# Cross-attention kernel: adding the mask and taking the minimum in one VectorE instruction per tile, instead of a mask matmul on TensorE

## The reference, cut to what matters

```python
q   = layernorm(x) @ Wq.T + bq                        # (32, 256, 16*64)
k   = concat([side @ Wk.T + bk, ctx @ Wgk.T + bgk])   # 512 keys
v   = concat([side @ Wv.T + bv, ctx @ Wgv.T + bgv])
att = einsum('bhqd,bhdk->bhqk', q, k) / sqrt(64)
att[..., :256] = where(mask, -inf, att[..., :256])
x   = x + (softmax(att) @ v) @ Wo.T + bo
x   = x + fp8_quantised_gemm(layernorm(x), ffn_kernel) + ffn_bias
```

## Time and profile before

| | us | share of the span |
|---|---|---|
| median of 3 executions (lowest, highest) | 2909.78 (2906.48, 2913.43) | |
| span of the profiled execution, first to last instruction | 2906.8 | |
| PE busy | 2793.8 | 96% |
| PE weight load busy | 2431.0 | 84% |
| DVE busy | 2315.1 | 80% |
| POOL busy | 2099.0 | 72% |
| ACT busy | 1982.3 | 68% |

### The profile page before, as it was taken

The page is one execution under the profiler, slowest core; times in us unless marked ns, Lnnn a source line. Parts: engine busy times, 40 slices in busy tenths (PEclk is TensorE's granted clock), DMA queues, the critical chain, the costliest instruction groups (busy, mean ns, idle before and its releaser), DMA issues.

```text
span 2906.8 us, 68146 instructions
## 1 busy us (share of the span) xinstructions
PE 2793.8 (96%) x20352; PEld 2431.0 (84%) x20352; DVE 2315.1 (80%) x3793; ACT 1982.3 (68%) x4742; POOL 2099.0 (72%) x2504
## 2 busy tenths in 40 slices
PE   5999999999999999999999999999999999999997
PEld 4888888888888888888888888888888888888886
DVE  5888778888778887788887788877888877888776
ACT  4666676766677666767666776667676667766674
POOL 4777777777768777777777687777777776877775
PEclk9999999999999999999999999999999999999998
DMA  5333333333333333333343333333333433333331
GB/s 170 82 77 90 76 86 82 80 79 91 72 90 87 76 90 76 87 83 79 79 92 71 90 87 76 90 77 86 85 79 78 93 69 90 87 76 90 78 82 37
DMA packets 176029, 243.02 MB, mean 84 GB/s; under 512 B 25472, under 2 KB 92544, under 8 KB 176000
## 3 DMA queue, kind: packets, MB, share of 16 engines
q1 hardware_dynamic: 176000, 242.66, 35.6%
HBM read 66.40 MB, written 8.39 MB: 26 GB/s over the span
## 4 chain that ended last, share of the span: by engine, by line
PE 61%; DVE 17%; issue 13%; ACT 7%; DMA 1%; DVEq 1%; POOL 0%; SPq 0%; ACTq 0%; POOLq 0%
PE ps_misc L555 20%; PE ps_o L658 10%; PE ps_pt L645 10%; PE ps_misc L599 8%; PE ps_scores L631 5%; PE ps_scores L632 5%; DVE pt_lo L941 5%; DVE kv_out L912 3%; PE ps_scores L634 2%; ACT probs L786 2%; DVE q_lo L889 2%; DVE scr_b L875 1%; DVE o_t L949 1%; ACT zq_out L751 1%; DVE scr_a L877 1%
## 5 line engine op out<-in xcount | busy, mean ns | idle before, releaser
L481 POOL TENSOR_SCALAR probs<-probs,recips 128x512 f32<-128x512 f32 x1024 | 698.4, 694 | 457.0 <-DVE recips L936 456.8
L795 ACT CAST pt_hi<-ps_pt 128x512 fp32r<-128x512 f32 x1024 | 551.7, 595 | 319.8 <-PE ps_pt L645 314.5
L786 ACT ACTIVATE probs<-ps_scores,neg_max 128x512 f32<-128x512 f32 x1024 | 696.0, 688 | 23.5 <-DVE neg_max L932 11.4
L941 DVE TENSOR_TENSOR pt_lo<-ps_pt,pt_hi 128x512 fp32r<-128x512 f32 x1024 | 655.2, 680 | 53.2 <-ACT pt_hi L795 50.3
L932 DVE TENSOR_REDUCE neg_max<-ps_scores 128x2 f32<-128x1024 f32 x512 | 621.1, 1213 | 9.5 <-PE ps_scores L634 9.5
L658 PE MATMUL ps_o<-pt_hi,v_hl 128*128 128x256 f32 x2048 | 554.6, 302 | 1.0 <-DVE o_t L949 1.0
L645 PE MATMUL ps_pt<-ident,probs 128*128 128x128 f32 x4096 | 531.5, 273 | 1.6 <-DVE pt_lo L941 1.6
L658 PE MATMUL ps_o<-pt_lo,v_hl 128*128 128x256 f32 x2048 | 511.4, 281 | 0.0
L645 PEld LDWEIGHTS ps_pt<-ident,probs 128*128 128x128 f32 x4096 | 464.5, 141 | 8.6 <-POOL probs L481 2.0
L631 PE MATMUL ps_scores<-k_hl,q_hh 128*128 128x512 f32 x1024 | 456.8, 446 | 9.0 <-issue 4.7
L632 PE MATMUL ps_scores<-k_hl,q_lo 128*128 128x512 f32 x1024 | 407.1, 398 | 0.0
(11 more groups left out here) (106 smaller groups left out, 6567.1 us busy)
## 6 DMA issues: line engine op xcount, KB each, us to landing
k_hl<-k_split SPq DMA_DIRECT2D x1024, 128.0 KB, 2.3
mask_sb<-mask_dram SPq DMA_DIRECT2D x128, 256.0 KB, 3.3
q_hh<-q_hh SPq DMA_DIRECT2D x256, 128.0 KB, 2.4
x_sb<-x_dram SPq DMA_DIRECT2D x32, 256.0 KB, 2.8
side_raw<-side_t_dram SPq DMA_DIRECT2D x32, 256.0 KB, 3.6
scr_b<-ctx_t_dram SPq DMA_DIRECT2D x32, 256.0 KB, 2.8
out_dram<-y SPq DMA_DIRECT2D x32, 256.0 KB, 2.1
probs<-wq_t_dram SPq DMA_DIRECT2D x1, 1024.0 KB, 5.1
```

The source lines that it names most:

```text
L481: nc.gpsimd.tensor_scalar(probs[:, h % 2, t, :], probs[:, h % 2, t, :], recips[:, h % 2, t:t + 1], 1.0, ALU.mult, ALU.mult).then_inc(norm_ ...
L786: nc.scalar.activation(probs[:, h % 2, t, :], ps_scores[:, h % 2, t, :], ACT.Exp, bias=neg_max[:, h % 2, t:t + 1], scale=-1.0, accum_out=s ...
L795: nc.scalar.copy(pt_hi[:, h % 2, 2 * k:2 * k + 2, :], ps_pt[:, k, :, :]).then_inc(pthi_done, 1)
L941: V.tensor_tensor(pt_lo[:, h % 2, 2 * k:2 * k + 2, :], ps_pt[:, k, :, :], pt_hi[:, h % 2, 2 * k:2 * k + 2, :].bitcast(F32), ALU.subtract). ...
```

## The change

The mask matmul, its weights and PE's waits for the mask are gone. The minimum is now taken by `tensor_tensor_reduce`, one instruction for each of the two query tiles: it reads the tile's scores (128x512 f32, PSUM) and 512 mask bytes (SBUF), computes `out = (in0 + in1) * MASK_STEP`, writes that back over the scores in PSUM, and writes the minimum of `out` and 3e38 to `neg_max`. For the keys without a mask the second input reads 256 bytes of zeros that stand in one new row behind the mask rows (a pattern of two rows, `row::MASK_ROWS - row`). `w_q` and its bias are scaled by -1/8 / 2**80, so that the instruction's factor 2**80 restores the scores while a mask byte becomes 2**80. `min_done` now rises twice per head, and ACT waits for it tile by tile. DVE waits for the mask of a group before the first head of it, and its wait for the scores stands apart.

```diff
@@ buffers
-        mask_weight = sb("mask_weight", [P, P], BF16)
-        mask_sb = sb("mask_sb", [P, 2, GH * QT * S], U8)
+        mask_sb = sb("mask_sb", [P, MASK_ROWS + 1, S], U8)      # MASK_ROWS = 2 * GH * QT
-        W_SCALE = {"q": SCORE_SCALE}
+        W_SCALE = {"q": SCORE_SCALE / MASK_STEP}                # MASK_STEP = 2.0 ** 80
@@ SP: load_mask
-                    wait_apart(sp, "sp", scores_done, H * b + GH * (n - 1))
+                    wait_apart(sp, "sp", min_done, QT * (H * b + GH * (n - 1)))
@@ PE: scores
-                    mm(dst, q_lo[:, n % 2, i, rows], k_hl[:, n % 2, i, :], start=False, stop=False)
-                    m = mask_sb[:, n % 2, (i * QT + t) * S:(i * QT + t + 1) * S].bitcast(FP8E5)
-                    last = mm(dst[:, 0:S], mask_weight[:], m, start=False, stop=True)
+                    last = mm(dst, q_lo[:, n % 2, i, rows], k_hl[:, n % 2, i, :], start=False, stop=True)
@@ PE: batch
-                            pe.wait_ge(mask_loaded[nxt % 2], 16 * (2 * bb + nxt // 2 + 1))
@@ ACT: exps
-                act.wait_ge(min_done, g + 1)
-                if free:
-                    act.wait_ge(pt_full, 2 * (g - 1))
                 for t in range(QT):
+                    act.wait_ge(min_done, QT * g + t + 1)
+                    if free and t == 0:
+                        act.wait_ge(pt_full, 2 * (g - 1))
@@ DVE: mins
-                dve.wait_ge(scores_done, g + 1)
-                V.tensor_reduce(neg_max[:, h % 2, :], ps_scores[:, h % 2, :, :], AX_X, ALU.min).then_inc(min_done, 1)
+                wait_apart(dve, "dve", scores_done, g + 1)
+                n, i = h // GH, h % GH
+                for t in range(QT):
+                    row = (n % 2 * GH + i) * QT + t
+                    s = ps_scores[:, h % 2, t, :].rearrange("p (k s) -> p k s", s=S)
+                    V.tensor_tensor_reduce(out=s, in0=s, in1=mask_sb[:, row::MASK_ROWS - row, :], scale=MASK_STEP,
+                                           scalar=SCORE_LIMIT, op0=ALU.add, op1=ALU.min,
+                                           accum_out=neg_max[:, h % 2, t:t + 1]).then_inc(min_done, 1)
@@ DVE: prologue and batch
+            V.memset(mask_sb[:, MASK_ROWS, :], 0).then_inc(mask_zeros, 1)
-            V.tensor_scalar(mask_weight[:], ident[:], MASK_WEIGHT, None, ALU.mult)
+            dve.wait_ge(mask_zeros, 1)
+            dve.wait_ge(mask_loaded[0], 16)
+                        if (h + 2) % GH == 0:
+                            nxt = (h + 2) // GH % NG
+                            dve.wait_ge(mask_loaded[nxt % 2], 16 * (2 * (b + (h + 2) // H) + nxt // 2 + 1))
                         mins((h + 2) % H, g + 2)
```

More of the change, by code:

```diff
@@ L27 @@
 BF16 = mybir.dt.bfloat16
-FP8E5 = mybir.dt.float8e5
 U8 = mybir.dt.uint8
@@ L44 @@
 GW = GH * DK
+MASK_ROWS = 2 * GH * QT
 SCORE_SCALE = -1.0 / DK ** 0.5
 LN_EPS = 1e-5
-MASK_WEIGHT = 2.0 ** 116
+SCORE_LIMIT = 3.0e38
+MASK_STEP = 2.0 ** 80
 E4_MAGIC = 1.5 * 2.0 ** 20
@@ L221, in xattn_ffn_kernel @@
         zeros_done = sem("zeros_done")
+        mask_zeros = sem("mask_zeros")
         mask_loaded = [sem("mask_loaded0"), sem("mask_loaded1")]
@@ L302, in load_mask @@
                 if not (isinstance(b, int) and b == 0 and n < 2):
-                    wait_apart(sp, "sp", scores_done, H * b + GH * (n - 1))
+                    wait_apart(sp, "sp", min_done, QT * (H * b + GH * (n - 1)))
                 src = one(mask, b).rearrange("o p n -> (o p) n")
-                sp.dma_start(mask_sb[:, n % 2, :],
-                             src[:, n * GH * QT * S:(n + 1) * GH * QT * S]).then_inc(mask_loaded[n % 2], 16)
+                rows = mask_sb[:, n % 2 * GH * QT:(n % 2 + 1) * GH * QT, :].rearrange("p r s -> p (r s)")
+                sp.dma_start(rows, src[:, n * GH * QT * S:(n + 1) * GH * QT * S]).then_inc(mask_loaded[n % 2], 16)
             def one(ap, b):
@@ L678, in _ @@
             pe.wait_ge(q_placed, Q_PLACES)
-            pe.wait_ge(mask_loaded[0], 16)
             pe.wait_ge(consts_done, 1)
@@ L696, in batch @@
                         if ahead % GH == 0:
-                            bb = b + ahead // H
-                            pe.wait_ge(mask_loaded[nxt % 2], 16 * (2 * bb + nxt // 2 + 1))
                             pe.wait_ge(zq_ready, c.through("q", nxt, ZQ))
@@ L974, in _ @@
             dve.wait_ge(consts_loaded, CONSTS)
-            V.tensor_scalar(qk_bias[:, 0, :], qk_bias[:, 0, :], SCORE_SCALE, None, ALU.mult)
+            V.tensor_scalar(qk_bias[:, 0, :], qk_bias[:, 0, :], SCORE_SCALE / MASK_STEP, None, ALU.mult)
             V.reciprocal(scales[:, 2:4], scales[:, 0:2])
```

## The result

Before takes 2908.53 us (median, 2906.48 to 2913.43), the changed kernel 2924.78 us (2923.71 to 2925.53). The ratio is 1.0054, with an interval of 1.004 to 1.0068: 0.54% slower, 16 us. The forecast was 1.4% slower, 40 us. The sign is right, the size is off by a factor of 2.5, so the experiments went after the terms of the sum.

What follows compares the result with a forecast made beforehand. DVE's chain was taken to bound heads 3 to 10, PE mostly the rest. Per batch 8d - 0.90, with d = 0.27, gives +1.26 us; times 32, +40 us: 2950 us, 1.4% slower, range 2885 to 3020.

Steps and rivals of the forecast that it cites:

- What bounds the kernel: Steady batch: DVE's chain, 98% busy, sets the time in heads 3 to 10; PE is busy all of the rest.
- What is added on DVE: Per head, two new minimum instructions of 0.60 + 0.10 us each replace one reduce of 1.13 us.
- d: Excess on DVE of a head's two new minimum instructions over the old single reduce, forecast 0.27 us.
- The other edits I cost at nothing: Semaphore increment, mask waits on DVE, later mask load, ACT's earlier first exponential, edits outside the loop: 0 us.
- semaphore pair: DVE's separate wait for the scores with its semaphore increment: costed at nothing, in the range at 0.5 us a batch.
- PE's gain: Removed mask matmuls save 0.90 us a batch: 0.21 at head 14's transposes, 0.69 in heads 15, 0 and 2.
- A: Rival: DVE's new instruction brings out its minimum at no cost; 2899 us, or 2881 at the reduce's rate; chance 0.25.
- case of no change: DVE's excess per head between 0.09 and 0.135 us, so that the time doesn't move; chance 0.10.
- B: Rival: PE bounds throughout, DVE's chain has slack, all 118 us of mask matmuls come back: 2792 us; chance 0.04.
- C: Rival: on DVE the minimum's read waits for the main part to end; excess 0.57 per head, 3027 us; chance 0.16.
- D: Rival: the new DVE instruction runs at half rate; excess 2.05 us per head, 3406 us; chance 0.03.
- The signs: PE busy down over 100 us, batch about 90.0, (6,B) wait up some 2 us, new (9,B) wait, minimum distance 1.40.

Runs made afterwards that it cites:

- e1: Kernel before without its mask matmuls, the mask left out of the computation: 2886.47 us, ratio 0.9916.
- e2: Changed kernel with the mask matmuls put back on PE, so the mask is added twice: 2945.31 us, ratio 1.0122.
- e3: Kernel before with two extra 128x2 reciprocals on DVE behind the minimum, in heads 5 to 11 only: 2925.55 us, ratio 1.0057.
- e4: Kernel before with two extra 128x2 reciprocals on DVE behind the minimum, in the nine heads outside 5 to 11: 2910.64 us, ratio 1.0002.
- e5: Kernel before with DVE's wait for the scores set apart with its semaphore increment, instead of the plain wait: 2915.64 us, ratio 1.0028.
- e6: Changed kernel with DVE's waits for mask and scores, and the semaphore increment, put ahead of the reciprocal's own wait: 2908.61 us, ratio 1.0002.
- e11: Changed kernel with mask matmul and plain reduce again for heads 4 to 11, first output's copy moved from head 3 to 13: 2870.63 us, ratio 0.9861.
- e9: Kernel before with DVE's copy of the first output moved from head 3 to head 13: 2884.16 us, ratio 0.9912.

## Why the prediction was wrong in size and right in sign

**What bounds the kernel: right.** Heads 3 to 10 belong to DVE and the rest mostly to PE. e1 and e2 show it from both sides: the stretch takes 41.54 without the mask matmuls and 41.56 with them, and with the new instruction 42.84 either way. e3 against e4 shows it by place. PE's busy share of 96% said the opposite. (The prediction's "PE's 98% in that stretch" is a misreading: 36.98 of 38.62 is 96%, and the 98% is DVE's.)

**The sum: the step that failed is "What is added on DVE", the 0.10 us per tile for bringing the minimum out.** The prediction took 0.60 + 0.10 per tile and d = 0.27. The instruction's timeline gives 1.24 to 1.27 for the two tiles and d = 0.12 in each head: 0.60 to 0.62 for the first tile and 0.65 for the second, with the read inside. The price was taken from the reciprocal's 0.10 as if small instructions add up, and already e3's two reciprocals hold 0.13 together. The Trainium skill, "VectorE: DVE Perf Modes", section "Two Vector instructions with no wait between them", says that such an instruction is two, and the trace agrees (1024 rows of 140 ns). How long the second part holds DVE I took from the reciprocal, and that was four times too large: (1.25 - 1.20) / 2 = 0.025 instead of 0.10. Of 7 x 0.27 = 1.89 in the stretch, 0.85 came.

With d = 0.12 the prediction's own sum is 8 x 0.12 - 0.90 = +0.06 us a batch, 2 us: no change. That isn't what was measured either, and the right sign was in part luck: with the sizes as measured, the kernel is slower by a term that the prediction put at nothing. Two more terms were off:

**"The other edits I cost at nothing": wrong for the semaphore pair, and it seems for the mask's wait in head 6.** The ledger of DVE's starts in heads 3 to 9, before to after: minima 7.93 to 8.78, idle ahead of them 0 to 0.37 (0.08, 0.20 and 0.09 in heads 3, 6 and 8), reciprocals 0.65 to 0.81, all else -0.1 net. The sum is the +1.28 of the stage. The -0.1 is itself a sum of large terms that the prediction doesn't have: +0.44 for the three neighbours in head 3, -0.33 for the normalise in head 9, -0.12 for `q_lo` in head 7, -0.09 for the quantising in head 6. That they nearly cancel is chance. The range had an item for the semaphore pair (0.07 x 7, 0.5 a batch), and that was the better value. e5 shows the pair's cost alone, 7.7 us or +0.27 in the stretch; of the 16 us that e6 gives back, -0.55, only 0.17 is idle time that is gone. The Trainium skill, "VectorE: DVE Perf Modes", section "The DRAIN you can't avoid", reports a chain of eight copies where a semaphore after each one cost nothing. Whether it stood in an instruction of its own the page doesn't say. Here, in e5, a wait and an increment in instructions of their own did cost, and the measurement decides.

**PE's gain: 0.62 to 0.66 a batch instead of 0.90.** e1 has -0.39 and -0.23, after -0.37 and -0.29. By the starts of single heads, 15 and 0 gave about 0.25 each, head 2 only 0.14, heads 13 and 14 together about 0.08 in after. The reason there is the one named, `norm` of head 14 on POOL: in after it ends at 1557.39 and the transposes start at 1557.52, 0.13 later, where the prediction allowed 0.06 for the signal. Why head 2 gave less isn't shown.

```profile
1556.02 1.37 POOL L485 TENSOR_SCALAR probs<-probs,recips 128x512 f32<-128x512 f32 x2
1557.52 1.09 PE L647 MATMUL ps_pt<-ident,probs 128*128 128x128 f32 x8
```

Together: 7d 1.89 became 0.85, nothing for the pair and its neighbours became 0.43 (0.37 + 0.16 - 0.10), and -0.63 (the 0.90, less d in head 12) became -0.66. That is +0.62 for the forecast +1.26.

**The rivals.** A (d = 0.07) is nearer in d than the forecast and has the wrong sign, since it leaves out the waits. The measured 0.12 lies in the case of no change (0.09 to 0.135), which had 0.10, and the distance of 1.24 to 1.27 stands right at the mark of 1.24 below which A was to decide. B is refuted by e1. C and D didn't come: the main part takes 707 ns, near the 680 of `pt_lo`. The row that spoke for D, L882 at 1589 ns, was no rate of its kind: in after the same operation (L881) takes 722 ns, and L879, which took 698 as L880, takes 1532. The Trainium skill's rule on two SBUF sources that aren't bf16 ("Vector Engine (DVE) Microarchitecture Reference", section "Points that are easy to get wrong") isn't borne out by that 722 ns either; both sources there are the same SBUF tile, in f32.

**The signs.** PE's busy time fell by 68 us and not by over 100, with 1024 matmuls fewer. A batch lost 3.7 us of matmuls and became 0.60 longer, so by this estimate PE stood still 4.3 us longer; its recorded idle time grew by 2.67 only. The rest would lie under the recorded ends of the matmuls ahead of a wait, 284 ns long where the next one can start after some 120. PE's wait at (6,B) grew from 0.83 to 1.21 in this batch, not to 2; (9,B), for which a wait was forecast, has 0.07 on average; instead the wait in head 3 grew from 0.16 to 0.59, and head 5 has new ones of 0.65 together. They are waits for DVE's copy. At (8,A), two heads after (6,B), PE waits for ACT, 0.55 (0.31 in before). Here are (6,B), (8,A) and (10,A):

```profile
1519.31 0.39 PE L559 MATMUL ps_misc<-zt_hi,wq_hi 128*128 128x256 f32 x1 [1.21 <-DVE kv_out L911]
1527.30 0.39 PE L559 MATMUL ps_misc<-kv_hi,wk_hi 128*128 128x256 f32 x1 [0.55 <-ACT z L767]
1538.38 0.65 PE L622 MATMUL ps_misc<-ident,scr_a 128*128 128x128 f32 x4 [0.68 <-DVE kv_out L911]
```

Over the run PE's weight loads for these chunks waited 122.5 us for that copy, 52.4 before, and its matmuls 80.6, 32.7 before:

```profile
PEld ps_misc L559 <- DVE kv_out L911: 122.5, 159, 2.5
```

**What stays open.** Why the pair leaves DVE idle in heads 3, 6 and 8 and not in 4, 5, 7 and 9. In heads 3 and 6 the wait just ahead of it, on the exponentials or on an earlier result, is a live one, which fits a sequencer that isn't ahead of its engine; that is inferred from where the gaps stand. How much of head 6's 0.26 is the mask's wait is inferred too, from heads 3 and 8. After with a plain wait in place of the pair, and after without the mask's wait, weren't tried.

## What to carry to other kernels

Find the stretch in which the receiving engine is full before moving work to it. The same two small instructions cost nothing in nine heads and 16 us in seven (e4, e3), and the best kernel does the mask on whichever engine has room in each stretch (e11). Moving work off the chain that decides can be worth more than making work cheaper beside it: here the copy (e9) outweighed the whole change. Price a second small instruction by its distance from start to start, never by its duration, and put a wait that is surely satisfied, with its semaphore instruction, ahead of a wait that really waits, not behind it: in head 3, where the next wait lasts 1.05 us, that saved its 0.17; in heads 6 and 8, where it doesn't, the idle time only moved (e6).

## What the runs showed that I had not expected

- The accumulator's row (140 ns) starts with the instruction behind it, and a pair with two of them holds DVE 0.06 us longer than two plain reduces of the same size.
- A DVE instruction's duration can more than double with what POOL does beside it, so that a shift of 0.3 us changes the chain's length elsewhere. The copy of 64x256: 606 ns in before, 1246 in after, and there it starts as POOL splits v_hl; in before it started at 1495.06 and was as good as over when that split began, at 1495.60.

```profile
1501.77 1.61 POOL L479 TENSOR_TENSOR v_hl<-kv_out,v_hl 128x512 fp32r<-128x512 f32 x1
1502.25 1.27 DVE L1045 COPY o_t<-o_first 64x256 f32<-64x256 f32 x1
```

  In turn the normalise behind it fell from 955 to 653 ns. The instructions that change so read from SBUF alone; `pt_lo`, the value copy and the minimum, with an input in PSUM, stay within some 30 ns. The Trainium skill, "GPSIMD Engine Reference", section "Specifications", says that GpSimd shares its SBUF interfaces with VectorE and collides with instructions that read two SBUF inputs or are in a two-port mode; the rows agree. This is why a DVE chain is elastic: e3's neighbours gave 0.32 back, in e9 9 us more went than the copy held, and in after the shift in head 3 made three neighbours 0.44 longer.
